# Layer 0 of a four-layer graph kernel: relation counts summed as nodes x relations, turned once a tile, and VectorE building tables one slot further ahead

## What is computed

```python
rel_vec = rel_emb[rel_ids]                       # 64 relations
msg = (node_states[src] + rel_vec) @ W_msg.T + b_msg
agg = jax.ops.segment_sum(msg, dst, num_segments=n_nodes)
deg = jax.ops.segment_sum(jnp.ones((dst.shape[0],), node_states.dtype), dst, num_segments=n_nodes)
agg = agg / jnp.maximum(deg, 1.0)[:, None]
return node_states @ W_self.T + b_self + agg
x = _layernorm(x + ..., axis=-1)                 # around it
```

## Time and profile before

| | |
|---|---|
| median of 3 runs | 6277.53 us (6276.63 to 6278.22) |
| the profiled execution's own time | 6280.96 us |
| its span, first to last instruction | 6279.2 us |
| mean granted TensorE clock over the span | 0.949 |
| TensorE matmul busy | 5405.9 us (86%) |
| VectorE busy | 4634.8 us (74%) |
| ScalarE busy | 2130.0 us (34%) |
| GpSimd busy | 1589.7 us (25%) |

### The profile page before, as it was taken

How to read it: one execution, slowest core, us unless ns; L and a number is a source line. 1 busy time by engine, 2 the same in 40 slices (tenths; PEclk the granted TensorE clock), 3 DMA queues, 4 the chain that set the end, 5 groups by cost and what they waited for, 6 DMA issues and landing times. The chain is left out here.

```text
span 6279.2 us, 121898 instructions
## 1 busy us (share of the span) xinstructions
PE 5405.9 (86%) x44062; PEld 4327.7 (69%) x44063; DVE 4634.8 (74%) x11931; ACT 2130.0 (34%) x3318; POOL 1589.7 (25%) x1592
## 2 busy tenths in 40 slices
PE   4899999999998118999949999999499999986998
PEld 3777777777776116767649999999377777764666
DVE  7777777778777217788859999999455555556888
ACT  0111111111111004444413333333266666653665
POOL 0577777777777740000000000000000000000000
PEclk9999999999999559999969999999699999997999
DMA  2100000000000000000000000000000000000000
GB/s 77 24 2 2 2 2 2 2 2 2 2 2 2 2 34 4 1 1 2 1 3 1 1 1 1 1 1 1 2 1 1 1 1 1 1 1 2 7 7 10
DMA packets 60230, 33.57 MB, mean 5 GB/s; under 512 B 51583, under 2 KB 54097, under 8 KB 59598
## 3 DMA queue, kind: packets, MB, share of 16 engines
q1 hardware_dynamic: 8622, 22.14, 1.1%
q0 software_dynamic: 50176, 3.31, 0.8%
q10 hardware_dynamic: 1056, 2.86, 0.2%
HBM read 13.67 MB, written 14.54 MB: 4 GB/s over the span
## 5 line engine op out<-in xcount | busy, mean ns | idle before, releaser
L1376 ACT ACTIVATE gC<-qC 128x768 bf16<-128x768 f32 (+3 forms) x1960 | 1611.8, 823 | 1745.4 <-PE qC L1414 1740.2
L1515 PE MATMUL qO<-X,gC 128*128 128x384 bf16 x9604 | 1932.1, 326 | 8.6 <-ACT gC L1376 8.6
L607 POOL DMA_INDIRECT records<-rec,idx x1568 | 1580.6, 1008 | 520.1 <-issue 494.6
L70 DVE TENSOR_TENSOR g<-iota_b,recs 128x768 bf16<-128x768 bf16 (+3 forms) x1970 | 1196.9, 643 | 577.6 <-PE qC L1414 526.8
L1414 PE MATMUL qC<-g 128*128 128x128 bf16 (+1 forms) x12029 | 1204.5, 242 | 100.4 <-DVE g L70 57.4
L1414 PEld LDWEIGHTS qC<-g 128*128 128x128 bf16 (+1 forms) x12029 | 1070.8, 136 | 262.0 <-DVE g L70 68.6
L1515 PEld LDWEIGHTS qO<-X,gC 128*128 128x128 bf16 x9604 | 889.0, 98 | 458.3 <-ACT gC L1376 13.2
L401 DVE SCALAR_TENSOR_TENSOR junk<-pK,key,earlier 128x128 f32<-128x128 f32 (+3 forms) x1568 | 767.9, 546 | 34.8 <-issue 27.0
L511 PE MATMUL pG<-run,hT 49*128 49x98 f32 x3136 | 793.4, 432 | 0.0
L558 ACT ACTIVATE hT<-pT 49x512 f32<-49x512 f32 x393 | 232.1, 591 | 1553.4 <-PE pT L488 1553.4
L511 PEld LDWEIGHTS pG<-run,hT 49*128 49x128 f32 x3136 | 697.2, 324 | 71.0 <-issue 71.0
(11 more groups left out here) (278 smaller groups left out, 4093.0 us busy)
## 6 DMA issues: line engine op xcount, KB each, us to landing
records<-rec,idx POOLq DMA_INDIRECT x1568, 2.1
records<-null SPq DMA_DIRECT2D x31, 256.0 KB, 9.5
recs<-records SPq DMA_DIRECT2D x1, 4866.0 KB, 14.0
B<-in_x SPq DMA_DIRECT2D x1, 2744.0 KB
out<-B SPq DMA_DIRECT2D x7, 392.0 KB
ety<-in_edge_type ACTq DMA_DIRECT2D x2, 686.0 KB
esrc<-in_src SPq DMA_DIRECT2D x1, 686.0 KB
edst<-in_dst SPq DMA_DIRECT2D x1, 686.0 KB
```

Of the source, the lines that this page charges most:

```text
L70: return v.tensor_tensor(o.rearrange("p n (a b) -> p n a b", b=2), iota_b[:, 0:w].rearrange("p (a b) -> p a b", b=2).unsqueeze(1).broadcas ...
L607: gp.indirect_dma_start(rec_d, bass.IndirectOffsetOnAxis(ap=idx[:, k:k + 1], axis=0), rec[:, k, :], None).then_inc(s_sent[g % 2], 16)
L1376: act.activation(Cs[:, u % 2, 0:n, :], pC[u % 2][:, 0:n, :], ACT.Copy).then_inc(s_cs, 1)
L1515: mm = pe.matmul(pO[i % SUMS][:, 0:width], Cs[:, u % 2, j, :], x, start=first, stop=last)
```

## The change

The two operands of the relation counts change places: `h2` (128 wide) becomes the weights, `h3` the moving operand with 64 columns. `pR` then holds nodes x relations in place of relations x nodes. The product with `relw` needs relations in the partitions, so each tile's counts are copied (128 x 64), transposed by TensorE with an f32 identity, and copied again (64 x 128, `rel_n`). The transpose takes the place of the product in slot 0, and the product moves to slot 1, behind `table` of slot 2. `h3` is now 64 wide without a gap, and the memset that cleared its second half is gone. VectorE's `make` runs three slots ahead in place of two, and its `take` moves from slot 0 to slot 1.

```diff
+            AHEAD = 3 if mode == "relation" else 2
...
-                    h3 = spare[:, room:2 * room].rearrange("p (h n w) -> p h n w", h=NHB, w=P)
+                    h3 = spare[:, room:room + room // 2].rearrange("p (h n w) -> p h n w", h=NHB, w=P // 2)
...
-                        if mode == "relation":
-                            v.memset(h3, 0.0).then_inc(s_blank, 1)
-                            v.wait_ge(s_blank, 1)
...
-                                    make(i, q + 2)
-                                    if q == 0 and i > 0:
+                                    make(i, q + AHEAD)
+                                    if q == (1 if mode == "relation" else 0) and i > 0:
                                         take(i - 1)
...
@@ ScalarE
                                     if mode == "relation" and u == 0 and i > 0:
                                         relations(i - 1)
+                                    if mode == "relation" and u == 1 and i > 0:
+                                        relations_turned(i - 1)
...
-                            act.activation(rel_t[:, :], pR[0:REL, 0:P], ACT.Copy).then_inc(s_rel, 1)
+                            act.activation(rel_t[:, :], pR[:, 0:P // 2], ACT.Copy).then_inc(s_rel, 1)
+
+                        def relations_turned(i):
+                            act.wait_ge(s_relt, i + 1)
+                            act.activation(rel_n[:, :], pE[0:REL, 2 * P:3 * P], ACT.Copy).then_inc(s_reln, 1)
...
@@ TensorE
                                     table(i, u + 1)
                                     q, h = u // H, u % H
+                                    if mode == "relation" and u == 1 and i > 0:
+                                        relations(i - 1)
                                     if u == 0:
                                         if mode == "relation" and i > 0:
-                                            relations(i - 1)
+                                            turn_relations(i - 1)
...
-                                            pe.matmul(pR[:, 0:P], h3[:, q % NHB, j, :], h2[:, q % NHB, j, :], start=first, stop=last)
+                                            pe.matmul(pR[:, 0:P // 2], h2[:, q % NHB, j, :], h3[:, q % NHB, j, :], start=first, stop=last)
...
-                        def relations(i):
-
+                        def turn_relations(i):
                             pe.wait_ge(s_rel, i + 1)
                             if i >= 1:
+                                pe.wait_ge(s_reln, i)
+                            pe.transpose(pE[0:REL, 2 * P:3 * P], rel_t[:, 0:REL], ident_f[:, :]).then_inc(s_relt, 1)
+
+                        def relations(i):
+
+                            pe.wait_ge(s_reln, i + 1)
+                            if i >= 1:
                                 pe.wait_ge(s_total, 2 * i)
-                            pe.matmul(pE[:, 0:P + 1], rel_t[:, :], relw[:, :], start=True, stop=True).then_inc(s_relm, 1)
+                            pe.matmul(pE[:, 0:P + 1], rel_n[:, :], relw[:, :], start=True, stop=True).then_inc(s_relm, 1)
```

More of the change, by code:

```diff
@@ L867, in aggregate_own @@
                 total = sb(f"total{name}", [P, P], F32, c) if mode != "weighted" else None
-                rel_t = sb(f"rel_t{name}", [REL, P], F32, c) if mode == "relation" else None
+                rel_t = sb(f"rel_t{name}", [P, P // 2], F32, c) if mode == "relation" else None
+                rel_n = sb(f"rel_n{name}", [REL, P], F32, c) if mode == "relation" else None
                 WT = sb(f"nWT{name}", [P, max(nW, 1), P], F32, c)
@@ L907, in aggregate_own @@
                 SUMS = len(pO)
-                s_rel, s_relm = [sem(f"{n}{name}", c) if mode == "relation" else None for n in ("t_rel", "t_relm")]
-                s_blank = sem(f"t_blank{name}", c) if mode == "relation" else None
+                s_rel, s_relt, s_reln, s_relm = [sem(f"{n}{name}", c) if mode == "relation" else None for n in ("t_rel", "t_relt", "t_reln", "t_relm")]
                 s_total = sem(f"t_total{name}", c) if mode != "weighted" else None
@@ L987, in make @@
                                 if mode == "relation":
-                                    equal(v, h3[:, par, 0:n, 0:64], rel_p[:, own, :], n, 64)
+                                    equal(v, h3[:, par, 0:n, :], rel_p[:, own, :], n, 64)
                                 ins = equal(v, h1[:, par, 0:n, :], recs_h[:, own, H_SL:H_SL + 2], n, H * P)
@@ L1251, in batch @@
                                     halve(i)
-                        make(0, 0)
-                        make(0, 1)
+                        for q in range(AHEAD):
+                            make(0, q)
                         batch(0, None)
@@ L1394, in _ @@
                             relations(NT - 1)
+                            relations_turned(NT - 1)
                         for tl in range(G7):
@@ L1534, in _ @@
                         if mode == "relation":
+                            turn_relations(NT - 1)
                             relations(NT - 1)
```

## The result

The changed kernel takes 6259.85 us (median of 8 runs, 6255.92 to 6264.88), the kernel before 6277.43 us in the same comparison (6276.63 to 6278.54). The ratio is 0.9971, with a 95% interval of 0.9961 to 0.9981: 17.6 us faster, where 36 were forecast. 6259.85 lies inside the range of 6221 to 6263, and the direction is right, but the gain is a little under half of the forecast.

The account below looks back on a forecast made before the run. TensorE was taken to bound most tiles, VectorE positions 0, 4 and 5. Terms of 25.2 + 6.0 + 1.6 + 1.3 + 2.7 - 0.6 = 36.2 us saved gave 6241 us, range 6221 to 6263.

Parts of the forecast that it names:

- the forecast's mechanism: Whole kernel: the summed savings hold, 6241 us, with 6228 to 6256 as its own range; chance 0.68.
- The shorter matmul: TensorE's count pairs: 64 moving columns take 29 ns, saving 26 ns a pair, 1.27 us for a tile's 49 pairs.
- the rival that no step is shorter: Count pairs: the 64-column matmul still needs 44 or 55 ns; 6264 or 6280 us; chance 0.13.
- the one with the weight load: Count pairs: a 98 ns weight load shows, 43 ns worse a pair; about 80 us longer, 6358; chance 0.05.
- the one that all of it counts: Whole stage: all 2401 pairs give 26 ns, 62 us, some 66 with memset and tile 1; 6212; chance 0.08.
- The product: Relation product moved into slot 1: 0.5 us added a tile, 0.1 us saved between tiles, its input early enough.
- the rival of the stalling product: Slot 1: ScalarE's second copy comes late and TensorE waits in every tile; 7 us gain left, 6270; chance 0.06.
- The tiles bound by TensorE: 29 tiles (four positions in six groups, five plain tiles): 0.87 us saved each, 25.2 us.
- The tiles bound by VectorE: Positions 0, 4 and 5 of six groups: 0.1, 0.9 and nothing saved, 6.0 us in all.
- The gap behind `halve`: End of the VectorE-bound tiles: `halve` stands behind one more `make`, so TensorE idles up to 2 us.
- First tiles and end: Stage's edges: memset gone saves 1.6 us, tile 0 saves 1.3, tile 1 saves 2.7, the end loses 0.6.

Follow-up runs that it names:

- the wide counts: Changed kernel with 128 moving columns again for the counts and the memset back: stage 798.8 us, ratio 1.0038 to the kernel before.
- the gaps filled: Changed kernel with unread matmuls where TensorE only waits, before slot 7's sums of position 4 and position 6's transpose: stage 745.2 us, ratio 0.9950.
- the square later: Changed kernel with ScalarE's square in slot 7 of position 4 in place of slot 6: stage 743.0 us, ratio 0.9969.
- The two repairs of order: Changed kernel with the square in slot 7 of position 4 and `halve` before the last `make` at positions 0, 4, 5: stage 729.0 us, ratio 0.9930.
- the old counts: Kernel before, with 128 moving columns, and only VectorE's lead changed, to three slots from two: stage 778.8 us, ratio 1.0009.

## Why the prediction was wrong

- **The whole: inside the range, beside the mechanism's own.** 6259.85 lies within 6221 to 6263, but the forecast's mechanism had 6228 to 6256 for itself, and what lay above that was there for rivals that did not come true. That the time fell inside the range is luck.
- **The shorter matmul: right.** 0.03 us from line 1521 to 1522 and 26 ns a pair, by the profile and by the wide counts. The one-column matmul of the earlier trace rows was the right row; the rival that no step is shorter and the one with the weight load are out. So is the one that all of it counts: the gain was 17.6 us, not 66.
- **The product: right.** 0.5 us in slot 1, the gap between tiles 0.98 us for 1.0. ScalarE's copy was early enough: TensorE waited for `rel_n` twice in 49 tiles, 0.9 us in all, so the rival of the stalling product is out. The 0.1 us for a load that is not covered had no row behind it and came out all the same. A plain tile went to 13.25 for 13.27.
- **The tiles bound by TensorE.** 25.2 us were forecast. The five plain ones gave 4.4. The 24 others gave 6 x (0.41 + 1.18 + 0.88 + 0.34) = 16.9, so 21.3 in all. Position 3 gave what was counted and position 2 0.3 more. Position 6 gave 0.34 in place of 0.87 because of the clock: with the gaps filled it is 13.24. Position 1 gave 0.5 less than counted, and no edit made it shorter. Its rows name the cause, which no run tested: ScalarE.

```profile
2494.83 1.64 ACT L1284 ACTIVATE X<-B,nb,sd 128x128 f32<-128x128 f32 x4
2496.36 0.79 ACT L1374 ACTIVATE gC<-qC 128x768 bf16<-128x768 f32 x1
2497.05 1.26 ACT L1284 ACTIVATE X<-B,nb,sd 128x128 f32<-128x128 f32 x3
2498.21 1.53 ACT L1374 ACTIVATE gC<-qC 128x768 bf16<-128x768 f32 x2
...
2498.38 0.51 PE L1419 MATMUL qC<-X,g 128*128 128x128 bf16 x6
2499.06 0.20 PE L1521 MATMUL qR<-X 128*128 128x64 bf16 x1 [0.17 <-ACT gC L1374]
```

Four and then three of `node`'s activations (line 1284) stand ahead of two slots' copies. ScalarE works there without a pause, and TensorE now wants a copy every 1.50 us. The sums of these two slots start 0.64 and 0.68 us behind `table` in place of 0.35, 0.6 us together. The tile's bound is ScalarE for two slots, and the count took TensorE's gain as if it were alone.

- **The tiles bound by VectorE: the step that failed.** "Position 4 ... I take 15.75, 0.9 saved" was off: it took 17.32 on average, 0.66 more than before by the unrounded means. With positions 0 and 5 (0.14 saved, 0.34 lost) the term was 6.0 us saved in the forecast and is 5.2 us lost in the profile. The text named the case ("If `node`'s steps ran into ScalarE this would be nil") as a bound and went no further, and it gave no reason for leaving it there. The earlier trace rows had ScalarE busy for 8 of 16.7 us, which looks like room; but busy time says nothing of a queue that stands behind one late step, and the 2.52 us before the square stood in the trace of before. I followed the moved `make` to `halve` and to TensorE and not to the steps of `node` behind it on VectorE and from there to ScalarE.
- **The gap behind `halve`: seen but priced too low.** "TensorE idles up to 2 us at the end of these tiles" was right for position 5 (2.05 us). I gave it its own length and nothing for the clock that fell with it. With that gap alone, in the run with the square later, position 6 took 14.02 us for 13.24 with the gaps filled, 4.7 us over six groups. With both gaps filled, the one in position 4 included, 8.5 us came back.
- **First tiles and end.** Tile 1 saved 2.8 (2.7 forecast), tile 0 1.0 (1.3). From the last matmul of the stage before to the first `table` it is 25.2 us for 26.4, so the memset gave 1.3 (1.6). The end cost 0.6 (0.6).
- **The sum.** 21.3 - 5.2 + 1.0 + 2.8 + 1.3 - 0.6 = 20.6 us less; the marks themselves give 20.4 (19.1 in the stage, 1.3 ahead of it), and the rest is rounding. Ahead of the stage this execution was 2.3 us longer and behind it 2.1, which leaves the span's 16.0. I have no run that explains these 4.4 us; the changed kernel's runs spread over 9 us and those of before over 2, and that stays open too.

Of the 36.2 us forecast, 15.8 were missed in this account. The two repairs of order are worth 24.7, more than that, because they also shorten what the forecast took as given (position 4 at 14.74).

## What to carry to other kernels

When an engine is made to run further ahead, every step behind the moved work in its queue comes later, and each must be followed to the engine that waits for it and to what stands behind that wait in an in-order queue. One late side step (a square for the next layer) held up the copies that the main loop lives on. A wait of such a step that the trace already shows is the place to look first. A shorter instruction on the bound engine is worth its difference only where that engine is the bound; cut the profile at the loop's own marks and cost each kind of iteration by itself.

## What the runs showed of the hardware

- A matmul of 64 moving columns is followed after 0.03 us by one with fresh 128 x 128 bf16 weights, at the full clock; with 128 moving columns it was 0.06 us (2609.43 to 2609.49 in the earlier trace rows).
- After TensorE had stood for some 2 us (gaps of 2.48 and 2.05 us, and of 1.74 us on the old counts) the granted clock went to its lower level, 1.2 GHz, and a pair took 0.35 us in place of 0.19. It happened with old and new matmul lengths and not at every gap: with the second gap alone in every second group, and on the old counts five times at 1.74 us and once at 2.49. It did not happen at the gaps of 1.1 us that every group of the changed kernel has at the start of position 1, and not at all when matmuls of no use filled the two longer gaps. The Trainium skill (TensorE: Matmul & The Clock Gate, "Part 1: The HAM clock gate") has idle time of TensorE as what lowers its clock; the filled gaps agree.
- The kernel before took 6277 us on one chip and 7046 to 7149 on others, and the changed kernel's stage was the same to 1 us (753.7 and 752.9). The extra time lies ahead of the stage; I did not look for its cause.
